# Two experts' inputs by one-hot products instead of the scatter and reload, and a buffer for each of twenty expert output tiles

## What is computed

```python
logits = x @ router_w                    # x: layer-normed, 1024 tokens
combine, dispatch = _top2_gating(logits, capacity)     # capacity 320 rows for each expert
expert_in = jnp.einsum('nec,nh->ech', dispatch, x)
hmid = jax.nn.silu(jnp.einsum('ech,ehf->ecf', expert_in, w1) + b1[:, None, :])     # 128 -> 512
expert_out = jnp.einsum('ecf,efh->ech', hmid, w2) + b2[:, None, :]                 # 512 -> 128
y = jnp.einsum('nec,ech->nh', combine, expert_out)
shared = jax.nn.silu(x @ sw1 + sb1) @ sw2 + sb2
out = y + 0.1 * shared
```

## Time and profile before

| | us |
|---|---|
| median of 3 runs | 311.07 |
| lowest, highest | 310.2, 315.35 |
| the profiled execution | 308.85 |
| its span in the trace | 307.0 |
| mean granted clock of TensorE | 0.922 |

### The profile page before, as it was taken

The page is one execution under the profiler, slowest core; times in us unless marked ns, Lnnn a source line. Parts: engine busy times, 40 slices in busy tenths (PEclk is TensorE's granted clock), DMA queues, the critical chain, the costliest instruction groups (busy, mean ns, idle before and its releaser), DMA issues.

```text
span 307.0 us, 4197 instructions
## 1 busy us (share of the span) xinstructions
PE 258.0 (84%) x1641; PEld 138.5 (45%) x1641; DVE 119.6 (39%) x376; ACT 98.9 (32%) x153; POOL 75.2 (24%) x94
## 2 busy tenths in 40 slices
PE   1899999788798579999999759779686899999863
PEld 0344443235437316787884314323232434547542
DVE  2676424154471000011120984626132873392211
ACT  2212541652152002734320012252655010741540
POOL 1811400020227720145462170000027180000000
PEclk9999999999879859999999957999999956999995
DMA  7999500000001142000113100000000000000000
GB/s 239 403 408 221 132 0 2 0 0 3 0 9 55 52 123 71 2 30 20 33 33 108 51 0 0 2 0 0 3 0 0 0 2 0 2 0 2 0 36 34
DMA packets 13820, 15.94 MB, mean 52 GB/s; under 512 B 1303, under 2 KB 10906, under 8 KB 13802
## 3 DMA queue, kind: packets, MB, share of 16 engines
q1 hardware_dynamic: 12272, 12.86, 13.8%
q0 software_dynamic: 1152, 2.05, 2.1%
q10 hardware_dynamic: 378, 0.78, 0.8%
HBM read 10.74 MB, written 5.26 MB: 52 GB/s over the span
## 4 chain that ended last, share of the span: by engine, by line
PE 68%; DVE 14%; ACT 9%; issue 4%; DMA 4%; POOL 1%; SPq 0%; ACTq 0%; DVEq 0%; POOLq 0%
PE ts L706 9%; PE wk L483 7%; PE wk L741 7%; PE ts L589 6%; PE wk L549 5%; ACT pr L936 5%; PE wk L615 5%; PE wk L545 5%; DVE nmx L1073 4%; PE wk L713 2%; PE wk L506 2%; DVE xn L1060 2%; PE ts L592 2%; PE ts L579 2%; PE wk L630 2%
## 5 line engine op out<-in xcount | busy, mean ns | idle before, releaser
L1073 DVE TENSOR_REDUCE nmx<-wk 128x4 f32<-128x308 f32 (+1 forms) x94 | 46.0, 539 | 30.4 <-PE wk L549 24.4
L483 PE MATMUL wk<-bpk 128*128 128x512 bf16 x180 | 49.7, 431 | 6.6 <-issue 4.2
L936 ACT ACTIVATE pr<-ts 77x1024 f32<-77x1024 f32 x32 | 30.9, 1014 | 27.9 <-PE ts L594 14.8
L392 POOL TENSOR_TENSOR rstd<-ve,half 128x4 f32<-128x4 f32 (+1 forms) x8 | 9.6, 1205 | 114.0 <-DVE ve L1055 114.0
L483 PEld LDWEIGHTS wk<-bpk 128*128 128x128 bf16 x180 | 18.3, 106 | 37.0 <-issue 15.6
L440 POOL DMA_INDIRECT y_d<-onT,dst_i x20 | 19.4, 971 | 34.7 <-DVE onT L1296 20.6
L545 PE MATMUL wk<-w,qT 32*128 32x512 f32 x60 | 20.7, 747 | 3.3 <-DVE nmx L1073 1.9
L741 PE MATMUL wk<-w,pr 128*128 128x128 f32 (+1 forms) x192 | 22.0, 278 | 0.0
L996 ACT ACTIVATE pr<-ts,pk 128x320 f32<-128x320 f32 x32 | 16.5, 529 | 16.4 <-PE ts L706 16.2
L741 PEld LDWEIGHTS wk<-w,pr 128*128 128x128 f32 (+1 forms) x192 | 20.6, 173 | 2.8 <-issue 2.0
L433 POOL DMA_INDIRECT xs_d<-xn,slot_i x16 | 15.8, 988 | 14.4 <-DVE slot_i L1252 9.8
(11 more groups left out here) (184 smaller groups left out, 345.4 us busy)
## 6 DMA issues: line engine op xcount, KB each, us to landing
w<-in_w SPq DMA_DIRECT2D x8, 512.0 KB, 11.6
xs_d<-fill SPq DMA_DIRECT2D x1, 1290.0 KB, 18.4
pr<-xs_d SPq DMA_DIRECT2D x5, 258.0 KB, 4.3
y_d<-fill SPq DMA_DIRECT2D x1, 1024.0 KB, 20.6
y<-y_d SPq DMA_DIRECT2D x4, 256.0 KB, 3.9
pk<-in_pk SPq DMA_DIRECT2D x1, 942.0 KB, 8.4
x<-in_x SPq DMA_DIRECT2D x2, 256.0 KB, 5.7
sw<-in_sw SPq DMA_DIRECT2D x2, 256.0 KB, 7.9
```

What stands on the lines that cost most here:

```text
L483: pe.matmul(w, onesb, bpk[:, 0:S].bitcast(BF16), start=True, stop=True)
L936: m = act.activation(prs[u][0:NK, r, 2 * i:2 * i + 2, :], ts[0:NK, 2 * i:2 * i + 2, :], ACT.Exp)
L1073: v.tensor_reduce(dst, src, AX.X, ALU.max, negate=True).then_inc(job_dve, 1)
```

## The change

For experts 0 and 1 (`PICKED` = 2) the inputs no longer come from `xg`. VectorE computes for each token its place in each of the two experts (`place`), and compares a constant row 0 to 319 (`places`, 320 more columns of the packed constants) with it: 16 comparisons of 128 x 320, one for each expert and group of 128 tokens, give one-hot matrices `oneh`. TensorE multiplies the tokens by them (`picked`: eight accumulating matmuls of 128 x 320 for each expert), and ScalarE copies the two products (`dx`) to `xgT`. All rows are still scattered and loaded, since the token numbers are needed, but the loads are cut otherwise (`XG_TILES`): tiles 0 to 4 come last and are no longer transposed. TensorE makes the hidden layers and the five output tiles of experts 0 and 1 ahead of `gathered`. The `keep_warm` ahead of it shrinks from 40 to 8. `ostage` has a buffer for each of the 20 tiles, 16 of them in the memory of `y12`, so VectorE no longer waits for a buffer. `oT` and `on` are put into one tensor `att`, whose memory the second `oneh` borrows.

```diff
@@ -67,3 +67,3 @@
         ("boA", P), ("sb2", P), ("boC", P), ("vbD", P), ("obD", P),
-        ("iota8", NT * E), ("tok", NT), ("sidx", ST)]
+        ("iota8", NT * E), ("tok", NT), ("sidx", ST), ("places", CAP)]
 PACK_AT, _at = {}, 0
@@ -74,2 +74,7 @@
 PACK_CUT = [0, PACK_AT["wqA"][0], PACK_AT["woA"][0], NPACK]
+PICKED = 2
+XG_TILES = [(5, 9), (9, 13), (13, 17), (17, 20), (0, 5)]
 
@@ -130,4 +135,6 @@
     add("dve", ("logits", 1), ("pos", 0), ("pos", 1), ("sh", 0), ("sh", 1))
-    add("act", *[("xg", n) for n in range(ST // 4)])
-    add("dve", *[("eo", i) for i in range(ST)])
+    add("act", *[("dx", e) for e in range(PICKED)])
+    add("dve", *[("eo", i) for i in range(5)])
+    add("act", *[("xg", n) for n in range(len(XG_TILES) - 1)])
+    add("dve", *[("eo", i) for i in range(5, ST)])
 
@@ -237,4 +244,5 @@
         pr = [sb(f"pr{i}", [P, 16 * S]) for i in range(2)]
-        oT = [sb(f"oT{b}", [P, 2, S]) for b in range(B)]
-        on = [sb(f"on{b}", [P, TB, D]) for b in range(B)]
+        att = sb("att", [P, B * 3 * S])
+        oT = [att[:, 2 * S * b:2 * S * b + 2 * S].rearrange("p (k n) -> p k n", k=2) for b in range(B)]
+        on = [att[:, 2 * S * B + S * b:2 * S * B + S * b + S].rearrange("p (t d) -> p t d", t=TB) for b in range(B)]
         onT = [sb(f"onT{b}", [P, S]) for b in range(B)]
@@ -250,3 +258,4 @@
         xgT = pr[1][:, ST * ROW:ST * ROW + SLOTS]
-        ostage = onT[0][:, :].rearrange("p (i d) -> p i d", d=D)
+        oneh = [t.rearrange("p (t n) -> p t n", t=NT) for t in (pr[1][:, ST * ROW + SLOTS:ST * ROW + SLOTS + NT * CAP], att[:, 0:NT * CAP])]
+        ostage = [y_flat[:, D * i:D * i + D] if i < 2 * NT else onT[0][:, D * (i - 2 * NT):D * (i - 2 * NT) + D] for i in range(ST)]
         prs = [pr[i][:, :].rearrange("p (r j n) -> p r j n", r=4, j=4) for i in range(2)]
@@ -313,3 +323,4 @@
         fill_src, fill_xs, fill_y, scat = (sem(n) for n in ("fill_src", "fill_xs", "fill_y", "scat"))
-        xg_in = [sem(f"xg_in{n}") for n in range(ST // 4)]
+        oh_ready = sem("oh_ready")
+        xg_in = [sem(f"xg_in{n}") for n in range(len(XG_TILES))]
         y_in = [sem(f"y_in{b}") for b in range(B)]
@@ -358,4 +369,4 @@
             xs_v = xs_d.rearrange("(i p) r -> p i r", p=P)
-            for n in range(ST // 4):
-                sp.dma_start(xg[:, 4 * n:4 * n + 4, :], xs_v[:, 4 * n:4 * n + 4, :]).then_inc(xg_in[n], 16)
+            for n, (lo, hi) in enumerate(XG_TILES):
+                sp.dma_start(xg[:, lo:hi, :], xs_v[:, lo:hi, :]).then_inc(xg_in[n], 16)
 
@@ -440,3 +451,3 @@
                 pool.indirect_dma_start(y_d, bass.IndirectOffsetOnAxis(ap=dst_i[:, i:i + 1], axis=0),
-                                        ostage[:, i % 4, :], None, bounds_check=2 * NTOK - 1, oob_is_err=False).then_inc(y_scats[i % 4], 16)
+                                        ostage[i], None, bounds_check=2 * NTOK - 1, oob_is_err=False).then_inc(y_scats[i % 4], 16)
 
@@ -716,9 +727,18 @@
 
+            def picked(e):
+                w = bank("dx", e)
+                for t in range(NT):
+                    pe.wait_ge(oh_ready, NT * e + t + 1)
+                    m = pe.matmul(w[:, 0:CAP], xn[:, t, 0:D], oneh[e][:, t, :], start=(t == 0), stop=(t == NT - 1))
+                m.then_inc(job_mm, 1)
             def gathered(n):
                 w = bank("xg", n)
+                lo, hi = XG_TILES[n]
                 if n == 0:
-                    keep_warm(w, 40)
+                    keep_warm(w, 8)
                 pe.wait_ge(xg_in[n], 16)
-                for j in range(4):
-                    m = pe.transpose(w[:, P * j:P * j + P], xg[:, 4 * n + j, 0:D], ident)
+                for i in range(lo, hi):
+                    m = pe.transpose(w[:, P * (i - lo):P * (i - lo) + P], xg[:, i, 0:D], ident)
                 m.then_inc(job_mm, 1)
@@ -728,3 +748,7 @@
                     pe.wait_ge(moe_in[1], 16 * (E // 2))
-                after("xg", (CAP * (e + 1) - 1) // 512)
+                if e < PICKED:
+                    after("dx", e)
+                else:
+                    last = (CAP * (e + 1) - 1) // P
+                    after("xg", next(n for n, (lo, hi) in enumerate(XG_TILES) if lo <= last < hi))
                 for c in range(FC):
@@ -812,7 +836,13 @@
             shared_out(1)
-            for n in range(ST // 4):
+            for e in range(PICKED):
+                picked(e)
+            for e in range(PICKED):
+                expert_hidden(e)
+            pe.wait_ge(moe_in[2], 16 * (E // 2 + 1))
+            for i in range(5):
+                expert_out(i)
+            for n in range(len(XG_TILES) - 1):
                 gathered(n)
-            expert_hidden(0)
-            pe.wait_ge(moe_in[2], 16 * (E // 2 + 1))
-            for e in range(E):
+            expert_hidden(PICKED)
+            for e in range(PICKED, E):
                 if e + 1 < E:
@@ -986,5 +1016,8 @@
                 act.activation(hs[:, c, S * b:S * b + S], ts[:, n % 4, :], ACT.Silu, bias=col(f"sb1_{c}")).then_inc(hid_act, 1)
-            for n in range(ST // 4):
-                copy_out(xgT[:, 512 * n:512 * n + 512], "xg", n)
+            for e in range(PICKED):
+                act.activation(xgT[:, CAP * e:CAP * e + CAP], job("dx", e)[:, 0:CAP], ACT.Copy).then_inc(job_act, 1)
             for e in range(E):
+                if e == PICKED:
+                    for n, (lo, hi) in enumerate(XG_TILES[:-1]):
+                        act.activation(xgT[:, P * lo:P * hi], job("xg", n)[:, 0:P * (hi - lo)], ACT.Copy).then_inc(job_act, 1)
                 if e >= 3:
@@ -1261,2 +1294,10 @@
 
+            own(v.tensor_tensor(place[:, 0, :, :], hot[:, 0, :, 0:PICKED], hot[:, 1, :, 0:PICKED], ALU.add))
+            own(v.tensor_tensor(place[:, 1, :, :], rt[:, 0, :, 0:PICKED], rt[:, 1, :, 0:PICKED], ALU.add))
+            own(v.scalar_tensor_tensor(place[:, 0, :, :], place[:, 0, :, :], -1.0, place[:, 1, :, :], ALU.add, ALU.add))
+            for e in range(PICKED):
+                for t in range(NT):
+                    v.tensor_scalar(oneh[e][:, t, :], pack("places"), place[:, 0, t, e:e + 1], None, ALU.is_equal).then_inc(oh_ready, 1)
             own(v.scalar_tensor_tensor(g12[:, :, :], k12[:, :, :], 0.0, g12[:, :, :], ALU.is_equal, ALU.mult))
@@ -1282,17 +1323,20 @@
 
-            for n in range(ST // 4):
+            def add_bias(i):
+                w = job("eo", i)
+                k, r = 2 * (i // 5), i % 5
+                if r == 2:
+                    v.tensor_tensor(ostage[i][0:64, :], w[0:64, 0:D], b2[0:64, k, :], ALU.add)
+                    m = v.tensor_tensor(ostage[i][64:P, :], w[64:P, 0:D], b2[64:P, k + 1, :], ALU.add)
+                else:
+                    m = v.tensor_tensor(ostage[i], w[:, 0:D], b2[:, k + (r > 2), :], ALU.add)
+                m.then_inc(job_dve, 1)
+            v.wait_ge(moe_in[2], 16 * (E // 2 + 1))
+            for i in range(2):
+                add_bias(i)
+            for n in range(len(XG_TILES)):
                 v.wait_ge(xg_in[n], 16)
             v.scalar_tensor_tensor(dst_i[:, :], n1s[:, :], float(NTOK), xg[:, :, D], ALU.mult, ALU.add).then_inc(dst_ready, 1)
-            v.wait_ge(moe_in[2], 16 * (E // 2 + 1))
-            for i in range(ST):
-                w = job("eo", i)
-                if i >= 4:
-                    v.wait_ge(y_scats[i % 4], 16 * (i // 4))
-                k, r = 2 * (i // 5), i % 5
-                if r == 2:
-                    v.tensor_tensor(ostage[0:64, i % 4, :], w[0:64, 0:D], b2[0:64, k, :], ALU.add)
-                    m = v.tensor_tensor(ostage[64:P, i % 4, :], w[64:P, 0:D], b2[64:P, k + 1, :], ALU.add)
-                else:
-                    m = v.tensor_tensor(ostage[:, i % 4, :], w[:, 0:D], b2[:, k + (r > 2), :], ALU.add)
-                m.then_inc(job_dve, 1)
+            for i in range(2, ST):
+                add_bias(i)
             v.wait_ge(*done("sh", 1))
```

More of the change, by code:

```diff
@@ L287, in build @@
         slot_i = sb("slot_i", [P, 2, NT], I32)
+        place = sb("place", [P, 2, NT, PICKED])
         n1s = sb("n1s", [P, ST])
@@ L1378, in layout @@
         "iota8": wide(np.tile(np.arange(E) - E, NT)), "tok": np.arange(NT)[None, :] * P + part[:, None],
-        "sidx": slot - CAP * (slot >= CAP),
+        "sidx": slot - CAP * (slot >= CAP), "places": wide(np.arange(CAP)),
     }
```

## The result

| | median, us | lowest to highest, us | runs |
|---|---|---|---|
| kernel before | 311.37 | 308.04 to 332.08 | 20 |
| changed kernel | 316.46 | 311.21 to 361.47 | 20 |

The ratio is 1.0127, with a 95% interval of 1.0081 to 1.0172: the changed kernel is 1.3% slower, within the 2% at which a difference counts, but more than its noise. The forecast was 303.3 us, and the range ended at 314.5. The profiled execution of the changed kernel took 314.0 us, its span is 312.2.

A forecast was written before the change was run, and what follows sets the result against it. TensorE's row of expert work was taken to bound block B; ending at 153.4 instead of 161.16, it saves 7.8 us, other parts nothing: 311.07 - 7.8 = 303.3 us, range 300.5 to 314.5.

The forecast's parts named there:

- The walk of TensorE's row: Block B's TensorE work from the shared expert's end, 102.80, to the last expert: end at 153.4 against 161.16, 7.8 us earlier.
- stretch: TensorE from 102.80 to 112.12, during GpSimd's token scatters: 9.3 us gave 2.4 us of work, idle time put down to "issue".
- third rival: Stretch was a chance event of the profiled execution; shared expert ends at 101.9, 302.4 us; counted to the forecast's 0.47.
- the first rival: The thin stretch stays under the new products: 8.9 us lost against 7.8 gained, 312.2 us; chance 0.35.
- The remark on the output scatters: Against the stretch staying: TensorE shows no such gap while GpSimd scatters the outputs from 129 on.
- The rival's price: Cost if the thin stretch stays in block B: 6.9 us lost plus 2.0 us of half clock, 8.9 us; chance 0.35.
- The half clock: TensorE's granted clock at half from 112 to 116 if the thin stretch stays: 2.0 us more.
- GpSimd held up: VectorE's 16 comparisons block GpSimd's scatters, which end 18.2 us later: 318.7 us; chance 0.10.
- The Trainium skill's rule: VectorE's two-port tensor-scalar holds ports GpSimd needs for DMA descriptors; whoever comes second waits for the whole instruction.
- The buffers: Twenty output buffers instead of a ring of four for VectorE: worth nothing by themselves.
- The eight `keep_warm`: Ahead of TensorE's transposes in block B: 1.7 us, now on the path and useless there.
- nothing hung on the stretch before the change: In the kernel before, TensorE's thin stretch in block B cost nothing, as the tokens came later still.

The follow-up runs named there:

- chip F: The chip of the last group, where the unedited changed kernel took 303.64 us against 310.54 for the kernel before, ratio 0.9773, without the stretch.
- e18: The changed kernel again, unedited, on chip F: 303.64 us against 310.54 for the kernel before, ratio 0.9773.
- e16: The changed kernel again, unedited, on chip E: 313.45 us, ratio 1.0049 to the kernel before.
- chip E: The chip of e16 (changed kernel, 313.45 us) and e17 (315.83 us), both with the stretch; the kernel before took 309.7 us there.
- e4: Changed kernel with 100 small memsets on GpSimd ahead of the scatters, moving GpSimd's own instruction fetch: 312.75 us, ratio 1.0105 to the kernel before.
- e5: Changed kernel with 10 wide and 24 narrow warming matmuls for 18 wide ahead of block B's second transposes, 32 TensorE instructions more: 313.46 us.
- e17: The kernel of e1 again, unedited, on chip E: 315.83 us, ratio 1.0205 to the kernel before.
- e7: Kernel before with only the change's twenty output buffers, VectorE's waits for the ring of four removed: 310.81 us, ratio 1.0033.
- e11: The kernel of e1 without the eight `keep_warm` ahead of the transposes: 302.87 us, ratio 0.9859 to the kernel before.
- e1: Changed kernel with 82 narrow warming matmuls for 18 wide ahead of block B's second transposes, 128 TensorE instructions more: 303.8 us, ratio 0.9899 to the kernel before.
- e6: Changed kernel with 12 of 16 token scatters, the last four left out with their tokens: 309.36 us.
- e14: Changed kernel with 256 small matmuls added at the program's start, ahead of transposes A 0: 338.74 us.
- e8: Changed kernel with 146 narrow warming matmuls for 18 wide ahead of block B's second transposes, 256 TensorE instructions more: 301.85 us; 311.94 when run again elsewhere.

## Why the prediction came out wrong

**The walk of TensorE's row held, where there is no stretch.** The forecast let the row begin at 102.80 and end at 153.4. On chip F the shared expert ends at 99.81 + 1.95 = 101.76, about as the third rival said (101.9), and the row ends at 146.65 + 5.44 = 152.09; from the products' start to the end it is 50.5 us, 50.6 in the forecast. The time there is 303.64 us, forecast 303.3, third rival 302.4. The products took 8.6 us, hidden layers 4.3, tiles 5.3, `keep_warm` 1.7: each term as worked out. That the times agree to 0.3 us is partly luck: the row ends 9.1 us earlier than in the trace of before, 1.3 us more than forecast, and the median on chip F is 6.9 us below the kernel before, 0.9 us less.

**The step that failed is the choice between the forecast and the first rival**, that is the start of that walk at 102.80 in a kernel whose trace shows TensorE thin from 102.80 to 112.12. The prediction saw the stretch and said that the case hangs on it. It gave it 0.35, because TensorE shows no such gap while GpSimd scatters the outputs. In the comparison of record, the stretch was there: the products ran from 111.57 instead of 102.80, the first 15 records at half clock, and the row ended at 166.1 instead of 153.4. Nothing in one trace could tell that it belongs to where the program runs: the rival should have been the likeliest case, since it was in the trace, and its absence was what needed a reason. The remark on the output scatters was true, but a weak reason: they come in bunches of two to five in that trace, not sixteen in a row.

**The rival's price was too small for the trace of record.** It was 8.9 us, for an end at 162.3; the row ended at 166.1. Against the forecast's row the products' main part starts at 111.57 instead of 103.07 (102.80 and one record of 4.31 / 16 = 0.27 us), which is 8.5 us where 6.9 were given: I had let the stretch do as much useful work as before, 2.4 us, and only one record of a product passed. The half clock: 15 records take 7.15 us (111.57 to 118.72) where they take 15 x 0.27 = 4.04 at full clock, 3.1 us more, where 2.0 were given. From 118.72 to the end it is 47.4 us, against 46.2 from 105.91 to 152.09 in e18: 1.2 us more, most of it the new wait of 0.97 us for ScalarE, which the prediction didn't have. Together 8.5 + 3.1 + 1.2 = 12.8. In e16, the same program with the stretch on chip E, that wait isn't there (16 records of hidden layers in one piece from 133.46, 4.74 us), and the row ends at 157.22 + 5.44 = 162.7, 9.3 us behind the forecast's: there the price of 8.9 holds, as in e4, e5 and e17, whose rows end at 162.4 to 163.3. So the trace of record is the worst of these by some 3 us.

**GpSimd held up.** Not seen. The comparisons took 0.33 us each (0.45 in the forecast, 1.14 in the rival), and the scatters beside them 1.03 us at most, for 0.97 alone. The Trainium skill's rule (SBUF — State Buffer, Who interferes with whom) may describe the few hundredths; its full price, one comparison's length for each scatter, did not appear here. Whether the comparisons ran in the mode that the rule is about, no trace shows.

**The rest.** The buffers are worth nothing alone (e7: 1.0033, its interval reaches to both sides of 1). The eight `keep_warm` are 1.7 us of row for nothing (e11 against e1: 1.7 us in the row, 303.8 to 302.87 in the median, on two chips without the stretch, so the 0.9 us of the medians is no measure). That nothing hung on the stretch before the change is right to within the 2.4 us by which TensorE's transposes came after the landing: the kernel before is the same within 2.3 us on all six chips. The range's upper end, 314.5, was 2 us short of the median, as the rival's price was too small.

**What stays open.** Shown: the same program has the stretch or not, together with all others of its group, and where it is, it ends within 2 us of the last scatter (e6 and the trace of record) and begins 11 to 12 us after the first one's start, also in e14, where that start is at 111.5. The beginning may as well be tied to the shared expert, which starts with the scatters; no run separates the two. Not shown: what differs between the groups. It may be the chip, or where the loaded program lies in memory; no run separates these. The hour is less likely: from A to F, in order of time, the stretch was absent, there, absent, there, there, absent. What TensorE waits for in the gaps is open, and so is whether others would wait as well: VectorE and ScalarE have next to nothing to do there. It isn't GpSimd's own fetch (e4), nor a fetch of TensorE inside the scatters by itself (e8, e18).

## What to carry to other kernels

An idle stretch that the profile puts down to nothing ("issue") is a fact of the trace until something shows otherwise: when a change moves work into it, price the case in which it stays, and ask what the kernel had in it before. Here it was filler, so 7 us of lost work cost 2.4 us at most; the change put the critical path there, and a gain of 2.3% (chip F) became a loss of 0.5% (chip E, within noise) to 1.3% (the comparison of record). And compare experiments only on one chip with the unedited kernel beside them: edits to TensorE's program seemed to remove the stretch until the same kernels ran on chips with it and without it.

## What the runs showed of the hardware

- TensorE can get on in steps of about 0.7 us or twice that (in the changed kernel's first trace groups of weight loads start at 102.36, 103.08, 103.79, 104.50 and 105.91) while GpSimd issues indirect DMAs every 1.28 us, with nothing in the profile that it waits for. In three groups this was so in all ten traces, in three others in none of the seven that could show it. The granted clock then falls to half: 0.50 from 103.8 to 117.5 us in that trace, and full from 88.6 to 170.5 in e18.
- The loss shows only if TensorE has work on the critical path there: 8.5 to 11 us for the changed kernel and e1; the medians of the one before differ by 2.3 us at most between the groups.
- The saving of 9.1 us in TensorE's row (161.16 to 152.09) arrives in the profiled execution of e18 as 2.7 us of span (307.0 to 304.3); its granted clock is half for 20.5 us after 170.5, against 10.2 us at the same place in the profiled run of before, and its six runs spread over 299.3 to 306.17 us with clocks of 0.942 down to 0.909. In e8, whose row ends at 152.07, the half clock there lasts 10.3 us, and the span is 300.0: 7.0 of the 9.1 us arrive. The slower of the two spans has 10.2 us more of half clock.
